# Output projection of a gated delta kernel in high and low parts, with a new order of work

## The reference

```python
qkv = silu(conv4(x @ Wqkv));  q, k, v = split(qkv);  z = x @ Wz      # 16 heads of 128
beta = sigmoid(x @ Wb);  g = softplus(x @ Wa + dt_bias) * -exp(A_log)
q, k = l2norm(q) * scale, l2norm(k)
for t in range(512):                                 # per head, state M is 128x128
    M = M * exp(g[t])
    M = M + outer(k[t], (v[t] - k[t] @ M) * beta[t])
    out[t] = q[t] @ M
out = out * rsqrt(mean(out * out) + EPS) * norm_w * silu(z)
return out.reshape(b, l, 2048) @ Wout                # summed over the heads
```

## Time and profile before

| | us |
|---|---|
| median of 3 runs | 2854.52 (2853.42 to 2854.96) |
| the profiled execution | 2854.09 |
| its span, first to last instruction | 2852.0 |
| PE busy | 2673.0 (94%) |
| DVE busy | 2272.5 (80%) |
| ACT busy | 2150.6 (75%) |
| POOL busy | 1907.4 (67%) |

### The profile page before, as it was taken

One profiled execution on the slowest core, in us unless ns is written; L12 is line 12 of the kernel. 1 busy time (PEld: TensorE's weight loads), 2 busy tenths in 40 slices (PEclk: granted clock), 3 DMA queues, 4 the chain that ended last, 5 costly groups with the idle time before them and its releaser, 6 DMA issues. The chain is left out here.

```text
span 2852.0 us, 70166 instructions
## 1 busy us (share of the span) xinstructions
PE 2673.0 (94%) x23604; PEld 2262.3 (79%) x23604; DVE 2272.5 (80%) x5006; ACT 2150.6 (75%) x7286; POOL 1907.4 (67%) x1707
## 2 busy tenths in 40 slices
PE   3399999999999999999999999999999999986998
PEld 2288888888888888888888888888888888873554
DVE  5588888888888888888888888888888888843433
ACT  2388888888888888888888888888888888861221
POOL 2267777787777777777777777787777777751000
PEclk9699999999999999999999999999999999987999
DMA  5322222222222222222222222222222222201000
GB/s 193 124 90 98 90 91 74 98 90 92 78 86 97 90 90 75 97 90 97 70 95 90 97 80 85 90 97 89 70 96 90 98 78 80 94 1 61 29 29 30
DMA packets 78568, 241.79 MB, mean 85 GB/s; under 512 B 8336, under 2 KB 21520, under 8 KB 61584
## 3 DMA queue, kind: packets, MB, share of 16 engines
q1 hardware_dynamic: 78224, 237.41, 23.6%
HBM read 223.75 MB, written 13.63 MB: 83 GB/s over the span
## 5 line engine op out<-in xcount | busy, mean ns | idle before, releaser
L740 DVE SCALAR_TENSOR_TENSOR conv<-pj,cw,conv 128x511 f32<-128x511 f32 (+2 forms) x1152 | 847.1, 744 | 54.3 <-ACT conv L615 40.3
L928 PE MATMUL pj<-xt,w_hi 128*128 128x512 f32 x2048 | 684.3, 415 | 23.3 <-DVE wo L734 23.3
L541 POOL TENSOR_TENSOR kq<-kq,cum 128x512 f32<-128x512 f32 x256 | 442.1, 1745 | 0.0
L570 POOL TENSOR_TENSOR inv<-inv,x 128x512 f32<-128x512 f32 x128 | 148.3, 1159 | 411.3 <-ACT inv L674 411.3
L928 PE MATMUL pj<-xt,w_lo 128*128 128x512 f32 x1024 | 404.7, 395 | 0.0
L928 PEld LDWEIGHTS pj<-xt,w_hi 128*128 128x128 f32 x2048 | 348.7, 190 | 69.5 <-DVE wo L734 23.7
L615 ACT ACTIVATE conv<-pj,cw 128x512 f32<-128x512 f32 x384 | 266.3, 693 | 124.3 <-PE pj L928 114.6
L817 DVE TENSOR_TENSOR y<-bk,mask 128x256 f16<-128x256 f32 x512 | 216.0, 422 | 166.8 <-PE bk L994 160.5
L577 POOL TENSOR_TENSOR attn<-attn,part 128x512 f32<-128x512 f32 x256 | 326.7, 1277 | 10.8 <-ACT part L697 10.8
L634 ACT ACTIVATE squares_out<-tr 128x128 bf16<-128x128 f32 x1024 | 273.7, 300 | 46.3 <-PE tr L935 46.3
L1074 PE MATMUL pj<-wo,yt 128*128 128x256 f32 x1024 | 284.0, 400 | 0.8 <-DVE yt L870 0.8
(11 more groups left out here) (160 smaller groups left out, 7505.4 us busy)
## 6 DMA issues: line engine op xcount, KB each, us to landing
xt<-xt_scratch SPq DMA_DIRECT2D x128, 1024.0 KB, 4.8
decay<-decay_scratch SPq DMA_DIRECT2D x128, 256.0 KB, 5.3
cum<-cumdecay_scratch SPq DMA_DIRECT2D x128, 256.0 KB, 5.5
w_raw<-in_w_heads SPq DMA_DIRECT2D x16, 512.0 KB, 7.3
xt_scratch<-xt_hi SPq DMA_DIRECT2D x8, 512.0 KB, 2.8
xt_scratch<-xt_lo SPq DMA_DIRECT2D x8, 512.0 KB, 3.8
res<-in_x SPq DMA_DIRECT2D x8, 512.0 KB, 4.7
out<-yo SPq DMA_DIRECT2D x8, 512.0 KB, 3.1
```

The source lines that it names most:

```text
L541: last = nc.gpsimd.tensor_tensor(part, part, of(cum, p)[:, :], ALU.mult)
L740: nc.vector.scalar_tensor_tensor(out=conv[:, i, j:SEQ], in0=pj[:, i % 2, 0:SEQ - j], scalar=cw[:, i, p // NSEQ, TAPS - 1 - j:TAPS - j], in ...
L928: last = nc.tensor.matmul(pj[:, i % 2, :], w[:, kt, cols], x_[:, kt, :], start=(n == 0), stop=(n == 3 * KT - 1))
```

## The change

The output weights are loaded per head into two alternating buffers and split into a high (float32r) and a low part by POOL. `gated` on DVE also multiplies by `norm_w`. ACT rounds its result to a high part, POOL forms the low part, and each chunk's product becomes three float32r matmuls of 256 columns. The order of the calls in the four engine loops is new; `correction`, `inverse`, `q_norm`, `squares` and others run at another place, partly an iteration later by the loop's count.

```diff
-    wo = buf(ctx, "wo", [P, HEADS, DM])
+    wo = [buf(ctx, f"wo{i}", [P, DM]) for i in range(2)]
+    wo_hi = [buf(ctx, f"wo_hi{i}", [P, DM], F32R) for i in range(2)]
+    wo_lo = [buf(ctx, f"wo_lo{i}", [P, DM], F32R) for i in range(2)]
+    yt_hi = buf(ctx, "yt_hi", [P, SEQ], F32R)
+    yt_lo = buf(ctx, "yt_lo", [P, SEQ], F32R)
...
# SP
+            sp.dma_start(wo[0][:, :], w_out[:, 0, :]).then_inc(wo_in, DMA)
...
+                if a % NSEQ == 3 and a // NSEQ + 1 < HEADS:
+                    head = a // NSEQ + 1
+                    sp.wait_ge(wo_split, head - 1)
+                    sp.dma_start(of(wo, head)[:, :], w_out[:, head, :]).then_inc(wo_in, DMA)
# POOL
+            def split_out(head):
+                if head < HEADS:
+                    pool.wait_ge(wo_in, DMA * (head + 1))
+                    wait(pool, outp[1], NSEQ * (head - 1))
+                    nc.gpsimd.tensor_copy(of(wo_hi, head)[:, :], of(wo, head)[:, :]).then_inc(wo_copied, 1)
+                    pool.wait_ge(wo_copied, head + 1)
+                    nc.gpsimd.tensor_tensor(of(wo_lo, head)[:, :], of(wo, head)[:, :], of(wo_hi, head)[:, :].bitcast(F32),
+                                            ALU.subtract).then_inc(wo_split, 1)
+            def low_y(p):
+                if real(p):
+                    wait(pool, yt_hi_ready, p + 1)
+                    wait(pool, outp[1], p)
+                    nc.gpsimd.tensor_tensor(yt_lo[:, :], yt[:, :], yt_hi[:, :].bitcast(F32),
+                                            ALU.subtract).then_inc(yt_lo_ready, 1)
# ACT
+            def high_y(p):
+                if real(p):
+                    wait(act, yt_ready, p + 1)
+                    wait(act, outp[1], p)
+                    nc.scalar.activation(yt_hi[:, :], yt[:, :], ACT.Copy).then_inc(yt_hi_ready, 1)
# DVE
-            for h in range(HEADS):
-                last = nc.vector.tensor_scalar(wo[:, h, :], wo[:, h, :], nw[:, 0:1], None, ALU.mult)
-            last.then_inc(scaled, 1)
...
-                    nc.vector.tensor_tensor(yt[:, :], flat(tr), of(gate, p)[:, :], ALU.mult).then_inc(yt_ready, 1)
+                    wait(dve, yt_lo_ready, p)
+                    nc.vector.scalar_tensor_tensor(out=yt[:, :], in0=flat(tr), scalar=nw[:, 0:1], in1=of(gate, p)[:, :],
+                                                   op0=ALU.mult, op1=ALU.mult).then_inc(yt_ready, 1)
# PE
-            pe.wait_ge(scaled, 2 + LEVELS)
+            pe.wait_ge(scaled, 1 + LEVELS)
...
-                        last = nc.tensor.matmul(pj[:, i, DM * (c % 2):DM * (c % 2) + DM], yt[:, chunk(c)],
-                                                wo[:, p // NSEQ, :], start=True, stop=True)
+                        for n, (y_, w) in enumerate(((yt_hi, high), (yt_hi, low), (yt_lo, high))):
+                            last = nc.tensor.matmul(pj[:, i, DM * (c % 2):DM * (c % 2) + DM], y_[:, chunk(c)], w,
+                                                    start=(n == 0), stop=(n == 2))
```

More of the change, by code:

```diff
@@ L467, in _ @@
             load_xt(0)
-            for dst, src in ((cw[:, :, :, :], conv_w), (nw[:, :], norm_w), (wo[:, :, :], w_out),
-                             (mask[:, :], masks)):
+            for dst, src in ((cw[:, :, :, :], conv_w), (nw[:, :], norm_w), (mask[:, :], masks)):
                 sp.dma_start(dst, src).then_inc(consts_in, DMA)
@@ L580, in _ @@
                 split(i, 0)
+            split_out(0)
             for a in range(PAIRS + LAST_STAGE):
                 head, slot = a // NSEQ, a % NSEQ
+                inverse(a - 3)
+                scale_k_tok(a - 1)
                 scale_b(a - 1)
                 unit_diagonal(a - 1)
-                scale_k_tok(a - 2)
+                low_y(a - 4)
                 out_norm(a - 4)
                 first_transpose(a - 1)
-                scale_kq(a - 1)
                 low_b(a - 1)
+                add(0, a - 4)
                 add(1, a - 4)
-                k_norm(a - 1)
-                inverse(a - 2)
-                add(0, a - 4)
                 if slot % 2:
                     split(slot // 2, head + 1)
+                if slot == NSEQ - 2:
+                    split_out(head + 1)
+                scale_kq(a - 1)
+                k_norm(a - 1)
         @block.scalar
         def _(act):
-            act.wait_ge(consts_in, 8 * DMA)
+            act.wait_ge(consts_in, 7 * DMA)
             nc.scalar.activation(ident16[:, :], ident4[:, 0, :], ACT.Copy).then_inc(scaled, 1)
@@ L701, in _ @@
             for a in range(PAIRS + LAST_STAGE):
+                squares(turned_q, 1, sums_q, a - 1)
+                activate(K, a - 1)
+                take(2, a - 2)
+                correction(a - 3)
+                state_input(3, a - 4)
+                squares(turned_k, 0, sums_k, a - 1)
+                take_k(a - 1)
                 activate(V, a - 1)
+                state_input(0, a - 3)
                 take_out(a - 4)
+                take_v(a - 1)
                 take(3, a - 2)
-                take_v(a - 1)
                 out_squares(a - 4)
+                high_y(a - 4)
                 high_b(a - 1)
@@ L867, in gated @@
                     wait(dve, gate_ready, p + 1)
-                    wait(dve, outp[0], p)
-                    wait(dve, outp[1], p)
-                    nc.vector.tensor_tensor(yt[:, :], flat(tr), of(gate, p)[:, :], ALU.mult).then_inc(yt_ready, 1)
+                    wait(dve, yt_lo_ready, p)
+                    nc.vector.scalar_tensor_tensor(out=yt[:, :], in0=flat(tr), scalar=nw[:, 0:1], in1=of(gate, p)[:, :],
+                                                   op0=ALU.mult, op1=ALU.mult).then_inc(yt_ready, 1)
             for a in range(PAIRS + LAST_STAGE):
                 convolve(V, 3, a - 1)
-                mask_level(3, a - 2)
+                norms(a - 1)
                 inverse_norm(a - 1)
                 decay_b(a - 1)
+                mask_level(3, a - 2)
                 state_scale(a - 1)
                 state(0, a - 3)
-                rhs(0, a - 2)
-                q_norm(a - 1)
-                decay_qk(a - 1)
+                gated(a - 4)
                 rhs(1, a - 3)
                 mask_level(4, a - 2)
-                gated(a - 4)
+                decay_qk(a - 1)
                 out_sums(a - 4)
+                rhs(0, a - 2)
                 mask_first(a - 1)
@@ L888, in _ @@
                 decays(a)
+                q_norm(a - 2)
                 mask_level(1, a - 1)
@@ L894, in _ @@
                 convolve(Q, 2, a)
-                mask_level(2, a - 1)
                 convolve(Q, 3, a)
                 convolve(K, 1, a)
+                mask_level(2, a - 1)
                 convolve(K, 2, a)
+                convolve(K, 3, a)
                 state(2, a - 3)
-                convolve(K, 3, a)
                 residual(a - 2)
@@ L1072, in out_project @@
                         wait(pe, part_taken[i], p)
+                    high, low = of(wo_hi, p // NSEQ)[:, :], of(wo_lo, p // NSEQ)[:, :]
                     for c in (2 * i, 2 * i + 1):
[L1074 to L1075 removed]
+                        for n, (y_, w) in enumerate(((yt_hi, high), (yt_hi, low), (yt_lo, high))):
+                            last = nc.tensor.matmul(pj[:, i, DM * (c % 2):DM * (c % 2) + DM], y_[:, chunk(c)], w,
+                                                    start=(n == 0), stop=(n == 2))
                     last.then_inc(outp[i], 1)
             for a in range(PAIRS + LAST_STAGE):
+                outputs(0, a - 4)
+                solve(3, a - 4)
+                turn_k(a - 1)
+                grams(a - 1)
+                solve(0, a - 3)
                 outputs(3, a - 4, signal=o_done)
+                z_level(3, a - 2)
+                turn_v(a - 1)
                 state_update(0, a - 3)
                 tx_level(3, a - 2)
[L1082 removed]
+                from_state_k(1, a - 3)
+                turn_o(a - 4)
+                z_level(4, a - 2)
                 project(Z, a - 1)
[L1084 to L1086 removed]
                 solve(1, a - 3)
[L1088 to L1089 removed]
                 tx_level(4, a - 2)
                 z_first(a - 1)
+                state_update(1, a - 3)
                 out_project(0, a - 4)
[L1093 to L1094 removed]
                 z_level(5, a - 2)
@@ L1097, in _ @@
                 tx_level(5, a - 2)
+                z_level(1, a - 1)
                 project(Q, a)
                 z_level(6, a - 2)
+                from_state_k(2, a - 3)
                 tx_level(1, a - 1)
-                from_state_k(2, a - 3)
                 project(K, a)
@@ L1105, in _ @@
                 tx_level(6, a - 2)
+                out_bank_free(a - 3)
                 outputs(1, a - 3)
-                tx_level(2, a - 1)
[L1108 to L1113, removed]
-                correction(a - 2)
[L1115 to L1119, removed]
+                project(V, a)
+                turn_q(a)
+                state_update(2, a - 3)
+                residual(a - 2)
```

(4 more changed lines are left out.)

21 lines of the change are left out of this document (7 added, 14 removed).

## The result

The changed kernel took 3062.03 us (median of 4 runs, 3060.93 to 3063.81), the kernel before 2853.97 beside it (2852.97 to 2854.96): a ratio of 1.073, 95% interval 1.0711 to 1.0748. The profiled execution took 3063.81 us (span 3061.9), 0.06% above the median, so its rows can stand for it.

The account below looks back on a forecast made before the run. PE was taken to set the time: its list of 18.18 us plus waits of 0.35, 0.5 and 1.35 gives 20.38 us a pair. 2854.1 + 187 - 6 + 2 = 3037 us, range 2990 to 3090 (8 in 10: 2800 to 3090).

Parts of the forecast that it names:

- block of six matmuls: Output product on PE, each half: six float32r matmuls of 256 columns in 0.83 us, against 0.92 and 0.95 before.
- PE's list: PE's work in a pair without waits: from 18.39 to 18.18 us, with the bounds 18.0 to 18.36.
- pair: One loop iteration over a (head, sequence) pair: 20.38 us against 18.87, 1.51 more, in 124 iterations +187 us.
- Products: Six matmuls a half in the output product: 0.83 us, between bounds of 0.73 (everything halves) and 0.92 (no gain).
- First wait: PE before from_state_k(1): chain from state_update(0) takes 0.88 us, list between 0.53; wait 0.35 us, bounds 0.2 and 0.5.
- Second wait: PE at out_project(0), partly z_first: chain from turn_o 3.4 us, list 2.87; wait 0.5 us, bounds 0.3 and 0.8.
- Third wait: PE before from_state_k(2): POOL holds DVE's scan and q_norm behind decays; wait 1.35 us, bounds 0 and 1.9.
- Outside the loop: Before the first projection: less weight loading and scaling, -6 us, bounds -1 and -8; in the drain +2 us.
- (a): Rival: POOL is not in q_norm's way, third wait only 0 to 0.3 us; 2889 us, 2850 to 2920; chance 0.18.
- (c): Rival: the edits cancel, (a) with six matmuls in 0.73 and first wait at lower bound; 2850 to 2860 us; chance 0.04.
- (b): Rival: order hides the waits, PE's list alone sets the time, yt_lo ready within 2.87 us of turn_o; 2790 us; chance 0.20.
- (d): Rival: with the waiting, PE's clock falls from 2.4 to 1.2 GHz in places; 3260 or 3100 us; chance 0.06.

Follow-up runs that it names:

- number 10: Old order with the new products, out_project one stage later, and DVE's rhs(0) moved behind out_sums: 2797.94 us, 0.9814 of the kernel before.
- number 11: The kernel before with one line moved, DVE's rhs(0) to behind out_sums, without the new products: 2831.6 us, ratio 0.9925.
- number 1: The changed kernel with one line moved, q_norm from behind decays to behind inverse_norm: 2939.58 us, 1.0308 of the kernel before.
- number 7: The changed kernel with q_norm moved behind inverse_norm and state(1) put ahead of mask_level(1): 2909.14 us, 1.0195 of the kernel before.
- Numbers 9: The changed kernel's products in the old order, out_project one stage later, high_y and low_y in rests of ACT and POOL: 2824.56 us, 0.9904 of the kernel before.
- number 6: The changed kernel's products in the old order, out_project at its old stage and place: 3098.49 us, 1.0856 of the kernel before.
- number 4: The kernel before with one line moved, q_norm from the end of the step to behind decays: 2926.49 us, ratio 1.0264.

## Why the prediction was right

3037 us were forecast, 3062 measured, by the cause named. The terms, forecast and measured, in us a pair; the waits at `from_state_k` include the 0.1 by which the step behind them is longer:

| term | forecast | measured |
|---|---|---|
| block of six matmuls | 0.83 | 0.83 and 0.81 |
| PE's list | 18.18 | 18.23 (20.55 less the waits) |
| `from_state_k(1)` | 0.35 | 0.42 (0.34 in the next pair) |
| `z_first` and `out_project(0)` | 0.5 | 0.54 |
| `from_state_k(2)` | 1.35 | 1.36 |
| pair | 20.38 | 20.55 |

- **Products.** The value between the bounds held; number 10 against number 11 gives 0.25 us a pair for a forecast of 0.21, with the two blocks at 0.80 and 0.79 us there.
- **First wait.** 1016.37 to 1017.14 is 0.77 from `state_update(0)`, better than the 0.88 of the drain. But the list between is shorter than taken too (0.45 for 0.53), and the matmul behind starts 0.1 late.
- **Second wait.** The chain was forecast at 3.4 us, and took 3.46. The list between, which I had at 2.87, took 2.92, so the wait came out at 0.54 for 0.5. Over half of it, 0.30, sits at `z_first`, where the prediction had part of it.
- **Third wait.** Each step came in the forecast order: `out_sums` held by `low_y`, `rhs(0)` in 0.34, the scan held for 0.6 by `first_transpose`, `low_b` ahead of `q_norm`. `q_norm`'s own share is 122 us (number 1), the swap of two instructions behind it is worth 30 more (number 7). What the 0.6 of the scan costs by itself was not measured. In number 1 `from_state_k(2)` is still 0.26 late, with the scan at 1.84 and `mask_level(1)` right behind it; in number 7 nothing is left of that, with the scan at 1.84 as well.
- **Outside the loop.** The first projection started at 105.49 against 110.07, 4.6 us for a forecast of 6. With 124 x 1.68 = 208 and the 2 us taken for the drain, which were not measured, that makes 206 of the 208 us measured.
- **Rivals.** (a) and (c) fell with `q_norm`'s 1.05 us. (b) named the right condition: with 2.87 us behind `turn_o` nothing of the chain would show. Numbers 9 and 10 met it with a stage instead of an order, and landed at 2825 and 2798, where (b) stood at 2790. (d) did not happen: the loop ran at 1.00. It does happen in number 6, where 2.0 us of waiting stand close together and the clock falls in 15 pairs.

The misses of size: the waits together were 0.12 us too small and the list 0.05, which makes 21 of the 25 us that were missing. The range of 2990 to 3090 was narrower than the bounds it was taken from: all of them at their upper end come to 18.36 + 0.5 + 0.8 + 1.9 = 21.56 us a pair, over 3180 us, and all at their lower end, with the third wait at nothing, to about 2800. That the time fell inside owes something to each term having come out close to the value taken for it.

## What to carry to other kernels

Where VectorE's and GpSimd's lists run side by side, look through the line views for small instructions whose median is several times their minimum (0.15 and 1.05, 0.34 and 1.21 here). Here each was held until a GpSimd instruction ended, and cost time where another engine was about to want what stands behind it: about its whole delay in number 1, some 0.6 us of 1.0 in number 4. Cure it by moving the instruction, or by an operand in PSUM. And when an edit makes a chain longer than the list that hides it, give its consumer a stage more rather than a new order: the order brought four waits, the stage none of its own.

## What the runs showed of the hardware that I had not expected

- A held instruction counts as busy: DVE's busy time rose by 191 us (2272.5 to 2463.5), with 16 instructions fewer; in the pair the largest part is `q_norm` at 1.05 for 0.15 us, `out_sums` at 0.87 for 0.15 and the scan at 1.84 for 1.34.
- A 128x4 `tensor_scalar` with one SBUF operand is held like one with two (median 1.06 us); the same arithmetic with the other operand in PSUM is not (0.126 at the median, 0.148 at most, in 128).
- POOL pays too: `low_b` takes 1.16 us (median) in number 10, where no scan meets it, and 2.08 in the changed kernel; the two instructions of `scale_kq`, issued while the scan runs in number 4, take 3.45 us there and 2.53 in the changed kernel. In these rows the instruction that is held is the one that was issued while the other engine's was running or already waiting.
- In number 6 the granted clock fell to 0.50 for 3.41 us fifteen times in the loop, each time within 0.9 to 2.2 us after a wait of 1.40 us; in the changed kernel, with 2.1 us of waiting a pair in four places, it never did.
